# The turning of key blocks in a paged attention stage: all eight transfers of a group issued by SyncE

## What is computed

```python
k_blocks = k_blocks.at[blk, :, off, :].set(k.transpose(0, 2, 1, 3))
v_blocks = v_blocks.at[blk, :, off, :].set(v.transpose(0, 2, 1, 3))
k_all = k_blocks[block_tables].transpose(0, 2, 1, 3, 4).reshape(Bx, G, -1, HD)
scores = jnp.einsum('bghtd,bgsd->bghts', qg, k_all) * SCALE
allowed = (kpos[None, None, :] <= pos[:, :, None]) & (kpos[None, None, :] > pos[:, :, None] - WINDOW)
p = jax.nn.softmax(jnp.where(allowed[:, None, None, :, :], scores, -jnp.inf), axis=-1)
o = jnp.einsum('bghts,bgsd->bghtd', p, v_all).reshape(Bx, H, Tx, HD)
```

## Time and profile before

| | |
|---|---|
| median of 3 runs | 962.8 us (959.43, 962.80, 963.14) |
| the profiled execution | 958.42 us, its span 956.6 us |
| mean granted TensorE clock over the span | 0.932 |
| PE busy | 839.4 us (88%) |
| DVE busy | 567.4 us (59%) |
| POOL busy | 380.4 us (40%) |
| ACT busy | 347.1 us (36%) |
| q0, share of 16 DMA engines | 18.0% |
| q1, share of 16 DMA engines | 26.2% |

### The profile page before, as it was taken

One profiled execution on the slowest core, in us unless ns is written; L12 is line 12 of the kernel. 1 busy time (PEld: TensorE's weight loads), 2 busy tenths in 40 slices (PEclk: granted clock), 3 DMA queues, 4 the chain that ended last, 5 costly groups with the idle time before them and its releaser, 6 DMA issues.

```text
span 956.6 us, 16539 instructions
## 1 busy us (share of the span) xinstructions
PE 839.4 (88%) x5239; PEld 680.0 (71%) x5239; DVE 567.4 (59%) x1659; ACT 347.1 (36%) x1007; POOL 380.4 (40%) x405
## 2 busy tenths in 40 slices
PE   1999998985899999695489989979989979999997
PEld 1787776754798998684378868867447747777786
DVE  5646888555487876279487979451553444444343
ACT  3333443433233333022376868402442222221311
POOL 7300436266466677766535540000175003334000
PEclk9999999987799999798598999959998989999999
DMA  9225112777877542824788875000523003331222
GB/s 355 64 105 160 50 41 79 305 223 210 227 203 233 165 130 66 336 96 120 155 168 180 161 167 210 2 1 1 181 101 129 24 17 93 105 103 58 89 85 91
DMA packets 68179, 126.43 MB, mean 132 GB/s; under 512 B 20224, under 2 KB 50265, under 8 KB 65455
## 3 DMA queue, kind: packets, MB, share of 16 engines
q1 hardware_dynamic: 46783, 75.49, 26.2%
q0 software_dynamic: 20800, 47.76, 18.0%
q10 hardware_dynamic: 512, 2.13, 1.0%
HBM read 87.39 MB, written 43.30 MB: 137 GB/s over the span
## 4 chain that ended last, share of the span: by engine, by line
PE 61%; DMA 16%; DVE 9%; issue 4%; ACT 4%; POOL 3%; SPq 3%; DVEq 0%; POOLq 0%; ACTq 0%
PE ps L470 18%; PE ps L807 11%; PE ps L838 7%; PE ps L817 3%; DMA big<-big 2%; DMA early<-newblk,new_i 2%; DMA big<-mid 2%; DMA early<-early 2%; PE ps L2277 2%; PE ps L828 2%; PE ps L2514 2%; PE ps L2559 1%; POOL sent_d L909 1%; PE ps L2410 1%; PE ps L2453 1%
## 5 line engine op out<-in xcount | busy, mean ns | idle before, releaser
L909 POOL DMA_INDIRECT sent_d<-mid,slot_i x88 | 98.0, 1113 | 114.3 <-DVE mid L629 64.6
L851 ACT ACTIVATE early<-ps 128x256 f32<-128x256 f32 x134 | 51.3, 384 | 176.5 <-PE ps L817 176.5
L838 PE MATMUL ps<-early 96*128 (+1 forms) x346 | 99.3, 388 | 0.2
L869 DVE TENSOR_TENSOR early<-early,ps 128x96 f32<-128x96 f32 (+1 forms) x134 | 37.3, 278 | 99.5 <-ACT early L857 79.5
L900 POOL DMA_INDIRECT back_d<-early,mid x78 | 77.5, 993 | 34.6 <-issue 27.6
L504 DVE TENSOR_TENSOR hidl<-work,hidh 128x512 fp32r<-128x512 f32 (+1 forms) x56 | 38.8, 692 | 84.5 <-ACT hidh L497 84.5
L807 PE MATMUL ps<-big,early 128*128 x380 | 82.0, 339 | 3.3 <-issue 1.9
L510 ACT ACTIVATE work<-ps 128x512 f32<-128x512 f32 (+1 forms) x56 | 33.4, 596 | 138.6 <-PE ps L470 138.4
L900 POOL DMA_INDIRECT back_d<-big,mid x39 | 38.4, 984 | 111.8 <-DVE big L883 105.9
L807 PEld LDWEIGHTS ps<-big,early 128*128 128x128 f32 x380 | 69.6, 198 | 10.5 <-issue 5.2
L838 PEld LDWEIGHTS ps<-early 96*128 96x128 f32 (+1 forms) x346 | 56.2, 194 | 3.8 <-issue 1.3
(11 more groups left out here) (440 smaller groups left out, 2096.0 us busy)
## 6 DMA issues: line engine op xcount, KB each, us to landing
mid<-sent_d SPq DMA_DIRECT2D x117, 130.0 KB
big<-back_d SPq DMA_DIRECT2D x8, 512.0 KB
mid<-back_d SPq DMA_DIRECT2D x8, 512.0 KB, 7.0
early<-back_d SPq DMA_DIRECT2D x16, 256.0 KB, 3.1
early<-in_w SPq DMA_DIRECT2D x3, 1024.0 KB, 11.8
big<-in_gate SPq DMA_DIRECT2D x1, 3072.0 KB, 11.0
big<-in_up SPq DMA_DIRECT2D x1, 3072.0 KB, 16.2
early<-in_gu SPq DMA_DIRECT2D x1, 2816.0 KB, 10.0
```

What stands on the lines that cost most here:

```text
L838: last = nc.tensor.matmul(ps[:, 6 + j % 2, 0:D], L.hTb[j % len(L.hTb)][0:f1 - f0, h * P:(h + 1) * P], L.down[0:f1 - f0, h, bass.ds(owners[ ...
L851: nc.scalar.activation(L.yTb[b % ring_y], ps[:, b % 2, 0:2 * P], ACT.Copy).then_inc(s["turn_sb"], 1)
L869: nc.vector.tensor_tensor(L.hb[j % ring_h], L.sgb[j % 2], ps[:, 2 + j % 2, F:2 * F], ALU.mult)\
L909: nc.gpsimd.indirect_dma_start(out=sent_d, out_offset=bass.IndirectOffsetOnAxis(ap=L.slot_i[:, i:i + 1], axis=0), in_=L.rows[c][:, t, n, : ...
```

## The change

The four transfers with h = 1 move from POOL's program into SP's, each right behind the one with h = 0 of the same sequence. Their completions count on the semaphores of SP's half (`into`), so `TURNED` doubles and `LATER` becomes 0; the waits that are left of POOL's half on `gone` are those for the gather. `turn_rows` is gone, and with it POOL's waits in it.

```diff
-        TURNED, LATER = 16 * BPT, 16 * BPT
+        TURNED, LATER = 2 * 16 * BPT, 0
...
-        FIRST_DONE = {name: 32 for name in FIRST}
-        FIRST_LATER = (("castb", 80), ("seggot", 48), ("sent", NCH * HALF_SENT + 16),
-                       ("sent_late", NCH * HALF_SENT + 16))
+        FIRST_DONE = {name: 48 for name in FIRST}
...
                     for q, name in enumerate(FIRST):
                         sp.dma_start(*rows_of(0, 0, q)).then_inc(s[name], 16)
+                        sp.dma_start(*rows_of(0, 1, q)).then_inc(s[name], 16)
                     continue
                 for q in range(BPT):
                     sp.dma_start(*rows_of(g, 0, q)).then_inc(s["into%d" % t], 16)
+                    sp.dma_start(*rows_of(g, 1, q)).then_inc(s["into%d" % t], 16)
...
-            def turn_rows(g):
-                t = g % TPC
-                pool.wait_ge(s["gone%d" % t], got_new(g))
-                if g >= KV2:
-                    pool.wait_ge(s["o_ps"], O_CREDIT + BPT * (g - KV2 + 1))
-                for q in range(BPT):
-                    pool.dma_start(*rows_of(g, 1, q)).then_inc(s["gone%d" % t], 16)
...
             nc.gpsimd.memset(Qbd, 0.0).then_inc(s["qzero"], 1)
-            pool.wait_ge(s["gone0"], got_new(0))
-            for q, (name, _) in enumerate(FIRST_LATER):
-                pool.dma_start(*rows_of(0, 1, q)).then_inc(s[name], 16)
-            turn_rows(1)
             old_rows(4)
             pool.wait_ge(s["qkv_end"], 1)
             nc.gpsimd.memset(pickw, 0.0).then_inc(s["qzero"], 1)
-            turn_rows(2)
             old_rows(5)
             new_rows(4)
             old_rows(6)
-            turn_rows(3)
             new_rows(5)
             old_rows(7)
             for g in range(6, NT):
                 new_rows(g)
-                turn_rows(g - 2)
                 if g + 2 < NT:
                     old_rows(g + 2)
-            turn_rows(NT - 2)
-            turn_rows(NT - 1)
```

More of the change, by code:

```diff
@@ L1198, in new_rows @@
                         pool.wait_ge(s[name], FIRST_DONE[name])
-                    for name, count in FIRST_LATER:
-                        pool.wait_ge(s[name], count)
                 elif g > TPC:
@@ L2360, in keys @@
                     pe.wait_ge(s[FIRST[q]], FIRST_DONE[FIRST[q]])
-                    pe.wait_ge(s[FIRST_LATER[q][0]], FIRST_LATER[q][1])
                 elif q == 0:
```

## The result

The changed kernel takes **993.25 us** (median of 5 runs, 986.79 to 1001.9) against 960.48 for the kernel before in the same measurement (5 runs, 952.5 to 963.14): a ratio of 1.0362, 95% interval 1.031 to 1.0414. It is 32.8 us slower, where I had forecast 12.2. All ratios leave out the executions that the chip ran in a slower state, while medians count them, so that the two can differ a little (in E4 the most). The profiled execution has a span of 991.4 us against 956.6.

What follows compares the result with a forecast made beforehand. Six DMA engines filled by SP's queue were taken to limit the attention stage: 12 x 10.25 + 4 x 7.55 = 153 us, +12.5 us. 958.4 plus 12.5 is 971; with the median's 4.4 above, 975 us, range 950 to 1000.

Steps and rivals of the forecast that it cites:

- The late half: Attention stage: of the two halves of the turn, SP's is waited for (14.6 us of PE), and the change doubles its queue.
- the first rival: Attention stage: POOL's half is the late one, so moving it to SP gains 14 us, 949 us; chance 0.18.
- POOL's 40 us: POOL's program: 40 us of issuing saved, costed at nothing because POOL waits for turned blocks.
- The even exchange: Attention stage: at 52 ns or a little less per packet compute covers the added transfers, no change, 963 us; chance 0.16.
- the sum per busy engine: Turn and gathers on one of six full DMA engines: 153 us over 16 groups, last group 12.5 us later.
- The price of a 1 KB piece, 59 ns: SP's queue: each 1 KB packet holds its engine 59 ns, taken between 52 and 63; 128 packets cost 7.55 us a group.
- The gathers add 2.7 us per group: Full engines: 2.75 gathered rows add 2.7 us in each of twelve groups, making 10.25 us instead of 7.55.
- the sum at 52 ns: Per-engine sum at the lower packet price: 9.4 us a group with gathers, 6.7 without, 140 us in all.
- Group 1's wait stays at 7.34 us: PE before group 1: the wait is unchanged, since some 15 us of work lie ahead of it in both kernels.
- The serial rival: SP's queue: issuing stays at 1.5 us a transfer, 12 us a group, +51 us, 1014 us; chance 0.08.
- The upper end of my range: Whole kernel: 1000 us, holding packet prices of 63 ns (+21) and 70 ns (+30), leaving out the serial case.
- the ring: Ring waits (`o_ps`): hold nobody, since compute waits for the turn and not the turn for it.

Runs made afterwards that it cites:

- E4: The kernel before with POOL's h = 1 half of the turn left out: 996.71 us, ratio 0.9877 to the kernel before.
- E1: The changed kernel with turn transfers reading constants from 96 or 80 partitions instead of 6 or 5 of the window: 1007.4 us, ratio 0.9997 to the kernel before.
- E6: The changed kernel with the window's rows reordered so a transfer reads partitions 4 apart instead of adjacent: 1006.88 us, ratio 1.0073 to the kernel before.
- E3: The changed kernel with the gather of old blocks fetching 4 rows instead of 44 from group 4 on: 1042.83 us, ratio 1.0391 to the kernel before.
- E10: The changed kernel with source rows 4 partitions apart and only 4 old rows gathered from group 4 on: 952.76 us, ratio 0.9959 to the kernel before.
- E5: The changed kernel run again unaltered, as reference on another chip: 1028.14 us, ratio 1.0288 to the kernel before.

## Why the prediction came out as it did

The direction was right, and so was where the time is lost. The late half is SP's, and the first rival (POOL's half closes the group, faster) falls. q1 stays at 29.3% with the turn alone, under the 0.37 that I gave; the DMA share falls, 0.80 to 0.55, in a slower stage; PE waits for turned blocks in most groups, 15 times; POOL's 40 us bought nothing. The even exchange did not come either. E1 with 9.7 engines agrees with the rule that I took from the Trainium skill, "DMA: Bandwidth & Descriptors", section "Why a DMA increments its semaphore by 16 and not by 1", on the number of engines.

The size was 32.8 us and not 12.2. **The step that failed is the sum per busy engine**, in the first two of these terms; a third reading failed beside it:

- *The price of a 1 KB piece, 59 ns, and a queue bound by it.* I took an engine's time per piece between 52 and 63 ns. Alone on the queue it is 73, outside both ends, and the engines are not even always in use (4.7 at a time), so that 128 x 0.073 = 9.3 us a group would still be too little. What is measured is a rate of about 64 pieces per us, which rises to 117 when only the source rows lie apart (E6): 704 / 64 = 11.0 us a group, where I had 10.25 with gathers and 7.55 without. Over 16 groups that is 176 us for the 153 of my sum, and the four groups that I counted without gathers have 14 of the 23 us between them: SP's last two groups take (625.35 - 603.57) / 2 = 10.9 us each, 3.3 more than my term.
- *The gathers add 2.7 us per group.* They added nothing that could be seen: without 28 of the 32 old rows of a group the stage is as long (E3), and the price of a piece fell as they came, from 73 to 64 ns, at one rate of pieces. With rows apart they add (E10), and my frame fits better there: from group 3 to group 10 E6's first sequences are (591.36 - 521.17) / 7 = 10.0 us apart, from 11 to 14 (620.63 - 598.32) / 3 = 7.4, the pace of compute, where the sum at 52 ns had 9.4 and 6.7.
- *Group 1's wait stays at 7.34 us.* It grew to 12.70. SP's queue is behind all through the stage, so this adds nothing to the end of it, but the reason that I gave was wrong. SP had 16 transfers to issue from 448.65 on, at 1.38 us each, so group 1's last goes out at 469.61 and not before 466.73. I had costed old blocks that come sooner and not the queue that starts full.

Rows 9 misled me: 110 pieces per us at 52 ns, in a kernel in which SP read only h = 0 rows, where each transfer begins 11 partitions after the last and leaves 5 between them. In the change an h = 1 transfer reads those 5 in between. That this explains the difference is argued and not tried by itself. Single groups of the changed kernel also go faster than 64 pieces per us (group 10's eight transfers were issued in 569.78 - 562.03 = 7.75 us), and I can't say why.

The serial rival (1.5 us a transfer, 12 us a group, +51) had the better numbers, 1.38 and 11.4, but the wrong cause: SP takes 0.74 us for the same transfers when the source rows lie apart (E6). The upper end of my range, drawn at 70 ns a piece, held the result by luck, since it came from the same sum with a dearer piece and not from a limit at the source. The weights of L1102, sent at 625.35 in place of 576.92, delayed nobody, and nor did the ring.

What stays open: the 30% that E6 does not give back, and whether ports that neighbours share or something else in the nearness of the rows slows them. With at most 5.5 engines the rule of six is still there, and E1, with both lifted, stands at 0.9997; these agree, but no run changed the number of engines alone.

## What to carry to other kernels

Before moving transfers between queues, look at where they read and write: how many DMA engines the shape gives, and how closely the partitions of one transfer and of its neighbours in the queue lie. Spreading the rows over the partitions was worth more here (0.9915, with no instruction moved between engines) than any share between the queues. The gain of that was read on one distance, 4. And price a queue from a stretch with the load that it will have: a mean share of 16 engines that is far from full, or a packet's time in a mixed stretch, says nothing of a limit at the source.

## What was not expected of the hardware

- Transfers inside SBUF from 5 or 6 neighbouring partitions each, one behind the other, went at 64 pieces of 1 KB per us whether gathers ran beside them or not; 4 partitions apart, the same transfers went at 117 alone and at 75 beside gathers.
- A piece's time on its engine is not a property of the piece: 73 ns and 64 ns at the same rate, 47 ns with rows apart, and 0.514 x 1600 / 8662 = 95 ns in E1 from 500 to 600 us, where 16 engines share the work and the gathers run beside it.
- A half that nobody is seen to wait for (0.7 and 0.3 us in rows 6) cost 12 us of the kernel (E4). That it does so through the engines and the source rows, which it shares with the other half, is argued.
- All eight transfers on POOL, with its queue at 84.6% of 16 engines, cost 1.06%; all eight on SP, with its queue at 25.6% in the same stretch of E5 (500 to 620 us), cost 2.88% on the same chip. The Trainium skill, "DMA: Bandwidth & Descriptors", section "Issuing engine by pattern", calls SyncE's path generally faster; for these few-partition transfers the measurement says the opposite.
